# W2 loaded by casting and accumulating transfers instead of a staging ring

## The reference

```
x = x + dequant(quant(x))              # 8 thresholds on |x| choose one of 8 (delta, zero point)
x = x + x @ W1[a_b].T                  # W1: 8 adapters of 1024 x 1024, a_b chosen per batch
x = x + x @ W2.T + 0.5 * (x @ A[l_b]) @ Bw.T    # W2: 1024 x 1024, the same for all batches
x = x + (x @ B3[a_b].T) @ A3[a_b].T    # rank 16
```

## Time and profile before

| | us |
|---|---|
| median of 3 runs | 487.14 |
| the runs | 483.98, 487.14, 487.15 |
| span of the profiled execution, first to last instruction | 481.9 |
| PE busy in it | 464.9 (96%) |
| VectorE busy | 419.4 (87%) |
| ScalarE busy | 358.6 (74%) |
| POOL busy | 45.5 (9%) |

### The profile page before, as it was taken

How to read it: one execution, slowest core, us unless ns; L and a number is a source line. 1 busy time by engine, 2 the same in 40 slices (tenths; PEclk the granted TensorE clock), 3 DMA queues, 4 the chain that set the end, 5 groups by cost and what they waited for, 6 DMA issues and landing times.

```text
span 481.9 us, 8215 instructions
## 1 busy us (share of the span) xinstructions
PE 464.9 (96%) x3184; PEld 424.7 (88%) x3184; DVE 419.4 (87%) x481; ACT 358.6 (74%) x383; POOL 45.5 (9%) x46
## 2 busy tenths in 40 slices
PE   3999869999999999999999999999999999999997
PEld 3969669898999989898999989898999989898995
DVE  5999999999999899989999899989999899989120
ACT  6979958678877879678877879678887879675011
POOL 1064000200002000200002000210003000100000
PEclk9999989999999999999999999999999999999999
DMA  7997214712335122712335122712335122702002
GB/s 282 407 415 258 113 34 149 294 54 97 131 127 212 44 95 97 294 44 103 131 120 218 44 89 101 294 44 103 131 101 237 44 86 104 294 2 88 1 1 87
DMA packets 17830, 67.07 MB, mean 139 GB/s; under 512 B 2576, under 2 KB 5904, under 8 KB 13712
## 3 DMA queue, kind: packets, MB, share of 16 engines
q1 hardware_dynamic: 17808, 66.81, 37.9%
HBM read 56.84 MB, written 9.96 MB: 139 GB/s over the span
## 4 chain that ended last, share of the span: by engine, by line
PE 90%; ACT 3%; DMA 3%; DVE 2%; issue 1%; POOL 1%; SPq 0%; DVEq 0%
PE x_bank L603 45%; PE acc L628 34%; PE acc L579 3%; PE x_bank L616 3%; PE acc L640 2%; PE acc L638 2%; DMA w1b<-w 2%; DMA rows<-own_rows 1%; ACT mask L344 1%; ACT w2h L400 1%; DVE y L460 1%; PE acc L567 1%; ACT tq L329 1%; PE acc L577 0%; ACT outb L404 0%
## 5 line engine op out<-in xcount | busy, mean ns | idle before, releaser
L603 PEld LDWEIGHTS x_bank<-x,w1b 128*128 128x128 f32 x2048 | 233.2, 193 | 8.2 <-issue 4.9
L603 PE MATMUL x_bank<-x,w1b 128*128 128x128 f32 x2048 | 234.8, 276 | 3.7 <-DVE x L475 3.7
L344 ACT ACTIVATE mask<-absx,negtop 128x1024 bf16<-128x1024 f32 x112 | 128.4, 1146 | 40.3 <-DVE y L460 39.5
L329 ACT ACTIVATE tq<-xin,magic,rdelta 128x1024 f32<-128x1024 f32 x128 | 157.0, 1234 | 0.6 <-DVE yhigh L526 0.3
L460 DVE COPY_PREDICATED y<-mask,uq 128x1024 f32<-128x1024 int16 x112 | 151.1, 1349 | 0.1
L439 DVE TENSOR_SCALAR tq<-tq,par 128x1024 f32<-128x1024 f32 x128 | 99.2, 775 | 3.7 <-DVE y L460 3.1
L448 DVE TENSOR_SCALAR uq<-tq,ylow,yhigh 128x1024 f32<-128x1024 f32 x112 | 92.3, 824 | 0.2 <-DVE y L460 0.2
L628 PE MATMUL acc<-w2h,x2h 128*128 128x512 f32 x256 | 80.9, 393 | 2.0 <-DVE x2l L481 2.0
L628 PE MATMUL acc<-w2h,x2l 128*128 128x512 f32 x256 | 79.9, 390 | 0.0
L628 PE MATMUL acc<-w2l,x2h 128*128 128x512 f32 x256 | 79.2, 390 | 0.0
L295 POOL TENSOR_TENSOR w1b<-w1b,eye 128x256 f32<-128x256 f32 x32 | 36.5, 1140 | 368.9 <-DMA w1b<-w 368.9
(11 more groups left out here) (57 smaller groups left out, 218.9 us busy)
## 6 DMA issues: line engine op xcount, KB each, us to landing
w1b<-w SPq DMA_DIRECT2D x32, 1024.0 KB, 6.7
xin<-x SPq DMA_DIRECT2D x16, 512.0 KB, 3.7
out<-outb SPq DMA_DIRECT2D x14, 512.0 KB, 2.8
w1b<-w2n SPq DMA_DIRECT2D x4, 1024.0 KB, 10.6
ring<-w2t SPq DMA_DIRECT2D x6, 512.0 KB, 6.7
ua<-e_dram SPq DMA_DIRECT2D x16, 128.0 KB, 2.5
ua<-w2t SPq DMA_DIRECT2D x2, 512.0 KB, 7.8
va<-la SPq DMA_DIRECT2D x8, 128.0 KB, 2.7
```

Source lines behind the costliest of these rows:

```text
L329: nc.scalar.activation(tq[:, n % TQ, :], flat(xin, c % UN), ACT.Identity, bias=magic[:, 0:1], scale=rdelta[:, g:g + 1]).then_inc(t_ready, 1)
L344: nc.scalar.activation(mask[:, n % MK, :], absx[:, :], ACT.Relu, bias=negtop[:, g:g + 1], scale=1.0).then_inc(mask_ready, 1)
L603: last = nc.tensor.matmul(x2_bank[2 * t + i][:, o % HALF * P:(o % HALF + 1) * P], w1b[:, o, at:at + P], x1[:, t, k, :], start=(o % HALF == ...
```

## The change

The staging ring and VectorE's part of the work on W2 go away.

- POOL, after the third pair of w2n has landed, issues eight transfers that read W2 as fp32 and write w2h as f32r (a cast in the transfer).
- POOL adds the identity to the diagonal block in w2h.
- ScalarE, at the same steps as before, writes the negative of w2h into w2l.
- POOL adds the identity to w2l's diagonal block, waits for that, and issues a transfer that adds W2 from HBM onto w2l (accumulate). What is left in w2l is the remainder.
- PE waits for w2h's diagonal, and for each w2l block's own transfer.
- POOL clears `ua` once at the start; SP's load of U waits for that instead of for VectorE.

POOL's queue now holds: eight casting transfers; then per w1 pair j its diagonal, the w2h diagonals 2j and 2j + 1, and, from j = 1 on, the remainders 2j - 2 and 2j - 1; last the remainders 6 and 7.

```
-        ring = sb("ring", [P, ST - 1, D])
...
-            def load_w2(k):
-                if k >= ST:
-                    sp.wait_ge(w2l_ready, k - ST + 1)
-                sp.dma_start(stage[k % ST], w2t[k, :, :]).then_inc(stage_in[k % ST], 16)
...
-            sp.wait_ge(w2l_ready, ST + 1)
+            sp.wait_ge(pads, 4)
             load_u(a0)
...
+            nc.gpsimd.memset(ua[:, :], 0.0).then_inc(pads, 1)
             pool.wait_ge(b_in, 64)
-            def w2_diagonal(k):
-                pool.wait_ge(stage_in[k % ST], 16 * (k // ST + 1))
-                diag = stage[k % ST][:, k * P:(k + 1) * P]
-                nc.gpsimd.tensor_tensor(diag, diag, eye[:, :], ALU.add).then_inc(w2_diag, 1)
+            def round_w2(k):
+                nc.gpsimd.dma_start(w2h[:, k, :], w2t[k, :, :]).then_inc(w2h_in[k], 16)
+
+            def w2h_diagonal(k):
+                pool.wait_ge(w2h_in[k], 16)
+                diag = w2h[:, k, k * P:(k + 1) * P]
+                nc.gpsimd.tensor_tensor(diag, diag.bitcast(f32), eye[:, :], ALU.add).then_inc(w2h_diag, 1)
+
+            def w2_remainder(k):
+                pool.wait_ge(w2_negated, k + 1)
+                diag = w2l[:, k, k * P:(k + 1) * P]
+                nc.gpsimd.tensor_tensor(diag, diag.bitcast(f32), eye[:, :], ALU.add).then_inc(w2l_diag, 1)
+                pool.wait_ge(w2l_diag, k + 1)
+                nc.gpsimd.dma_start(w2l[:, k, :], w2t[k, :, :], accum_op=ALU.add).then_inc(w2l_in[k], 16)
...
+            pool.wait_ge(w2g_in[2], 16)
+            for k in range(KT):
+                round_w2(k)
             for j in range(PAIRS):
                 w1_diagonal(0, j)
-                w2_diagonal(j)
-            for k in range(PAIRS, KT):
-                w2_diagonal(k)
+                w2h_diagonal(2 * j)
+                w2h_diagonal(2 * j + 1)
+                if j:
+                    w2_remainder(2 * j - 2)
+                    w2_remainder(2 * j - 1)
+            w2_remainder(KT - 2)
+            w2_remainder(KT - 1)
...
                     k = ACT_W2.index(n)
-                    act.wait_ge(w2_diag, k + 1)
-                    nc.scalar.activation(w2h[:, k, :], stage[k % ST], ACT.Copy).then_inc(w2h_ready, 1)
+                    act.wait_ge(w2h_diag, k + 1)
+                    nc.scalar.activation(w2l[:, k, :], w2h[:, k, :].bitcast(f32), ACT.Copy, scale=-1.0) \
+                        .then_inc(w2_negated, 1)
...
-                if n in DVE_W2:
-                    k = DVE_W2.index(n)
-                    dve.wait_ge(w2h_ready, k + 1)
-                    nc.vector.tensor_tensor(w2l[:, k, :], stage[k % ST], w2h[:, k, :].bitcast(f32),
-                                            ALU.subtract).then_inc(w2l_ready, 1)
...
-                        pe.wait_ge(w2h_ready, k + 1)
+                        pe.wait_ge(w2h_diag, k + 1)
...
-                        pe.wait_ge(w2l_ready, k + 1)
+                        pe.wait_ge(w2l_in[k], 16)
```

More of the change, by code:

```diff
@@ L42, in quantised_residual_adapter_stack @@
     LAST = B - 1
-    TQ, MK, ST = 4, 2, 4
+    TQ, MK = 4, 2
     ctx = ExitStack()
@@ L93, in quantised_residual_adapter_stack @@
         ycut = uq[:, 1, :]
-        stage = [ua[:, :]] + [ring[:, i, :] for i in range(ST - 1)]
         a3s = outb[:, 0, :]
@@ L115, in quantised_residual_adapter_stack @@
         w2g_in = [sem(f"w2g_in{j}") for j in range(KT // 2)]
-        stage_in = [sem(f"stage_in{c}") for c in range(ST)]
+        w2h_in = [sem(f"w2h_in{k}") for k in range(KT)]
+        w2l_in = [sem(f"w2l_in{k}") for k in range(KT)]
         u_in = sem("u_in")
@@ L138, in quantised_residual_adapter_stack @@
         out_ready = sem("out_ready")
-        w2_diag = sem("w2_diag")
+        w2h_diag = sem("w2h_diag")
+        w2l_diag = sem("w2l_diag")
         x2h_ready = sem("x2h_ready")
@@ L154, in quantised_residual_adapter_stack @@
         e_ready = sem("e_ready")
-        w2h_ready = sem("w2h_ready")
-        w2l_ready = sem("w2l_ready")
+        w2_negated = sem("w2_negated")
         block = ctx.enter_context(nc.Block())
@@ L227, in _ @@
                 load_w1(a0, j)
-                load_w2(j)
             sp.wait_ge(g_ready, 2)
@@ L232, in _ @@
             load_x(1, 0)
-            load_w2(4)
-            load_w2(5)
             sp.wait_ge(g_out, 16)
             load_v(a0, lab0)
-            load_w2(6)
-            load_w2(7)
             for h in range(EH):
@@ L309, in quantised_residual_adapter_stack @@
         ACT_E = (12, 13, 13, 14)
-        ACT_W2, DVE_W2 = (9, 10, 11, 12, 13, 14, 15, 16), (10, 11, 12, 13, 18, 19, 20, 21)
+        ACT_W2 = (9, 10, 11, 12, 13, 14, 15, 16)
         ACT_X2, DVE_X2 = (14, 16), (13, 15)
@@ L360, in round_v @@
                 else:
-                    act.wait_ge(pads, 3)
+                    act.wait_ge(pads, 4)
                 nc.scalar.activation(v_hl[:, :, 0:R2], va[:, :, :], ACT.Copy).then_inc(vh_ready, 1)
```

## The result

The changed kernel takes 493.12 us (median of 4, 491.47 to 495.95), the kernel before 485.56 us beside it (median of 4, 483.43 to 487.15): a ratio of 1.0164, interval 1.012 to 1.0208. The forecast was 493 and slower. The profiled execution took 491.47 us with a span of 489.4, 7.5 us over the span before. In every comparison here the runs of the kernel before fall into two groups, near 484 and near 487 us, and its profile (span 481.9) belongs to the lower one, so a ratio of medians and a difference of profiled spans can disagree by up to 3 us.

What follows compares the result with a forecast made beforehand. TensorE was taken as solid behind x1 of unit 1, which ScalarE's run from 28.65 us holds. First copy +4.5 and VectorE beside POOL +1.2 make +5.7 us on 487.14: about 493, range 487 to 502.

Steps and rivals of the forecast that it cites:

- rival A: W2's casts do not get in w1's way, first copy before 28.65 us: 485.7 to 487.5 us, chance 0.13.
- What bounds the kernel: TensorE works solidly behind x1 of unit 1 (65.4 us); the change is worth what it does to that moment.
- VectorE's removed work is worth 0: Four subtractions ahead of x1 (5.1 us) are covered by ScalarE's run, four behind (4.5 us) by PE's: 0.
- POOL's issue at 1.35 us: Each of POOL's eight casting issues takes 1.35 us, together 10.8; the last is out at 29.5 us.
- rival C: VectorE holds up POOL's issues, 2.15 us each, first copy at 38.2: about 498 us, chance 0.20.
- Equal shares for w1's first pair, landing at 30.8: W2's casts and w1's load share the DMA engines equally; ScalarE's first copy starts at 33.1, not 28.65: +4.5 us.
- Rival D: W2's transfers crowd w1 out or run slower for casting, w1 at 35.5 or later: 497.5 to 502 us, chance 0.18.
- What stood behind them (G's store, x, V, E) is asked for no later: hidden, 0: In SP's queue, transfers behind the eight removed W2 loads are issued no later, so the change there costs 0.
- Later gates of POOL's queue: Later w1 additions make PE wait 1.7 and 4.2 us, hidden with 2.9 us left; later W2 additions hidden.
- Accumulations hidden under 13 us: The fourth accumulating transfer, issued at 51.4, is wanted by PE near 64.4; up to 13 us is hidden: 0.
- VectorE beside POOL, +1.2 us: Remainders 5 to 8 stretch four to six VectorE operations in the 10.1 us chain to x1: +1.2 us (0 to 3).
- TensorE's clock unchanged: Half clock after PE's idle before x1 stays: 0; if POOL held PE so it arrives last, 1.7 us come back.

Runs made afterwards that it cites:

- experiment 6: Kernel before without VectorE's eight subtractions; first version clears w2l once on POOL: ratio 1.0012; second has no clearing, LOW products read w2h: 0.9971.
- experiment 3: Changed kernel without the eight accumulating transfers: ratio to before 0.9974; with casting transfers in their place: 1.0077.
- experiment 4: Changed kernel with POOL's queue reordered, all eight remainders behind the diagonals and a wait for V's loads: ratio to before 0.9995.
- experiment 5: Changed kernel with casts 4 to 7 issued only after G's store has landed: ratio to before 1.016.
- experiment 1: Changed kernel with V's rounding and splitting moved behind x2h in every batch: ratio to before 1.015; control, the same move in the kernel before: 1.0118.

## Why the prediction was right in its number, and where not, point by point

The number and the direction came out; the place was right, and the two terms that made up the number were not. By the prediction's own signs, ScalarE's first copy at 28.54 was the mark of rival A, whose condition (w1 unharmed, issues under 0.9 us) came true but whose time of at most 487.5 did not; VectorE did stand idle before the x2l (3.37 and 2.72 us), x1 came at 74.7 and not near 71, and no rival had V in it.

- *What bounds the kernel* held: PE is solid behind x1 of unit 1, before and after, and the result can be read off that one moment and the clock.
- *VectorE's removed work is worth 0* held, and experiment 6 shows it: its idle time before x2l is what was removed.
- *POOL's issue at 1.35 us* was mis-sized: 0.54 to 0.88 us, eight in 5.19 us (5.1 to 7.0 in the other runs that issue eight). POOL was free at 23.9, not 29.5. That is inside the bounds given (0.43 to 2.15) and near the lower one, so rival C falls. "SBUF — State Buffer" of the Trainium skill (the box on "DVE blocks DMA") says that GpSimd can't write descriptors while VectorE runs an instruction in its two-port mode. VectorE was busy without a gap there, with instructions of 0.8 to 1.3 us, and the eight issues took a fifth of the 25 us that the prediction had estimated from the page's pair of times.
- *Equal shares for w1's first pair, landing at 30.8* was the step that failed. It landed at 26.1, 8.5 us after issue instead of 8.0, and the W2 casts took the delay themselves, 8.8 us for the first, 21.1 for the last. The +4.5 us at the first copy measured -0.1 (+1.0 and +1.2 in the runs of experiments 3 and 4 without early accumulations). Rival D's "w1 crowded out" falls with it.
- *"What stood behind them (G's store, x, V, E) is asked for no later: hidden, 0"* was the other step that failed, and the costly one. I compared issue times and not landing times. V was in at 43.8 and used at 47.5: 3.7 us of cover, against four blocks cast ahead of G's store and 4.19 MB of accumulations beside V's own loads. It came at 56.4, and ScalarE stood 7.04 us. Experiments 3, 4 and 5 show the cause from three sides: hold back casts 4 to 7 and G's store is as fast as before; take away or delay the accumulations and V's loads are at 2 us.
- *Later gates of POOL's queue*: PE waited 0.8 and 0.9 us for w1 pairs 2 and 3 (1.7 and 4.2 forecast), hidden as said. ScalarE waited 0.5 us at the second copy and 1.45 at the fifth, where none was forecast. The second copy's cast landed late (POOL itself stood 2.85 us for it). The fifth had POOL's queue ahead of it: from 38.36 to 43.95 POOL worked almost without idle on the fourth diagonal, two remainders and w1's third addition. The prediction had the fifth diagonal out at 45.9, later than the measured 44.7, but had ScalarE come for it only at 47.4, some 4 us later than it did; in experiments 3 and 4, without early remainders in the queue, that wait is gone.
- *Accumulations hidden under 13 us* held for PE (7.1 to 9.5 us each, no wait for w2l). That they load the engines for everyone else was not in the sum.
- *VectorE beside POOL, +1.2 us*: from x2h to x1 it took 11.0 us against 10.7, +0.3, since only the last remainder (65.28 to 67.98) fell into that stretch. With the remainders gathered there (experiment 4) it was about 1.5, the size forecast.
- *TensorE's clock unchanged* was off by 1.6 us, in the direction named but not by the way named (POOL holding PE): PE's long idle moved ahead of the HIGH products.

The sum was 4.5 + 1.2 = 5.7; the profile has 0.5 + 1.45 + 7.04 + 0.3 at x1 and 1.6 back. A right total from terms that were not the right ones, and by luck: the forecast change of 5.7 us measured 7.5 in the spans and 7.6 in the medians, and 493 was met to 0.1 us because the kernel before, taken at 487.14, had a median of 485.56 in the comparison.

What stays open: why one stream beside SP's cost G's store and V's loads so much and W1's loads so little. By the kernel's access patterns G's store and vg move in pieces of 512 bytes and W1 in pieces of 4 KB or more. (x, in long pieces too, took 17.1 us instead of 7.2, but it lay behind G's store in SP's queue.) "DMA: Bandwidth & Descriptors" of the Trainium skill (section "Queues, rings and completion order") says that each engine takes turns between its queues a packet at a time. If short pieces make small packets, that would fit; it is argued and not shown, since no run here changed the length of a piece.

## What to carry to other kernels

When a change adds bytes to a stretch in which the DMA engines are full, or moves bytes forward in it, list every transfer that lands in that stretch with its landing time and its first use, not only those in the queue that changed; the victim is the small one with the thin cover. Look at which engine stands idle right before the bounding step: work taken from that engine is worth nothing until the engine it waits for is relieved. Here an arrangement that relieved it (copies behind x2h, V later, diagonals first) took the same change to a gain of 0.5%. A control for a rearrangement is worth a run: without it, experiment 1 would have blamed the change for what the moved steps did.

## What the runs showed of the hardware

An accumulating transfer holds the DMA engines longer than a cast of the same bytes: 224 against 341 GB/s with the engines full in both, while W1's plain loads and the casts together moved 416 GB/s (28 to 32 us of the changed kernel). A single 512 KB transfer took 7.1 to 9.5 us to land as an accumulation and 5.1 to 7.7 as a cast in its place.

A long POOL instruction stopped short ones of VectorE. In experiment 6's first version POOL clears w2l from 2.52 us on; here is POOL's row, and VectorE's rows from the same execution:

```profile
2.52 6.93 POOL L285 MEMSET w2l<- 128x8192 f32 x1
...
5.35 4.12 DVE L517 TENSOR_SCALAR ylow<-par 128x8 f32<-128x8 f32 x1
5.38 4.11 DVE L518 TENSOR_SCALAR yhigh<-par 128x8 f32<-128x8 f32 x1
9.53 0.17 DVE L521 TENSOR_TENSOR ylow<-ylow,par 128x8 f32<-128x8 f32 x1
```

Eight elements per partition took 4.12 us, until the clearing ended at 9.45, and the whole first stage moved with them (x1 of unit 0 at 37.9 instead of 33.5 in the second version). The maximum and the reciprocal just before, beside the same clearing, took 0.17 and 0.18 us. "SBUF — State Buffer" of the Trainium skill ("Who interferes with whom") has the rule: VectorE's two-port instructions and GpSimd's exclude each other for a whole instruction, and whoever starts first holds the ports they share. The rows agree, in the direction in which VectorE is the one that waits; the page counts tensor_scalar among the instructions that can run in the two-port mode, and no row here shows a mode.
